# Normalising x on ScalarE instead of VectorE in the attention rounds of an attention and soft-mixture-of-experts kernel

## The reference

```python
def _layernorm(x, axis=-1, eps=1e-05):
    m = jnp.mean(x, axis=axis, keepdims=True)
    v = jnp.var(x, axis=axis, keepdims=True)
    return (x - m) / jnp.sqrt(v + eps)

# attention on the normalised x; each row of the scores is divided by its own length
qkv = einsum('bnm,om->bno', xn, w_qkv)
dots = einsum('bhid,bhjd->bhij', q, k)
attn = dots / max(sqrt(sum(dots * dots, -1)), 1e-12) * norm_g + norm_b
out = einsum('bhij,bhjd->bhid', attn, v) @ w_out.T + b_out
x = x + _layernorm(out)
x = x + _layernorm(soft_moe(_layernorm(x)))
```

## Time and profile before

| what | value |
|---|---|
| runs, us | 905.89, 907.99, 1957.71 |
| median, us | 907.99 |
| span of the profiled execution, us | 906.5 |
| PE busy, share of the span | 95% |
| DVE busy | 69% |
| ACT busy | 55% |
| attention rounds 2 to 6, length of each, us | 20.96 |

### The profile page before, as it was taken

How to read it: one execution, slowest core, us unless ns; L and a number is a source line. 1 busy time by engine, 2 the same in 40 slices (tenths; PEclk the granted TensorE clock), 3 DMA queues, 4 the chain that set the end, 5 groups by cost and what they waited for, 6 DMA issues and landing times.

```text
span 906.5 us, 15936 instructions
## 1 busy us (share of the span) xinstructions
PE 860.1 (95%) x5336; PEld 761.2 (84%) x5336; DVE 629.0 (69%) x1368; ACT 499.3 (55%) x875; POOL 131.4 (14%) x107
## 2 busy tenths in 40 slices
PE   5999999878999999997999999999999999998895
PEld 4888888766888888886899999999999999998895
DVE  4888888668989899998454545453535453479997
ACT  5433333226767667776655555555555554566652
POOL 0011111114322333324000000000000000014422
PEclk9999999969999999999999999999999999999998
DMA  7011120004222222222320202020202020067652
GB/s 245 1 48 47 46 69 23 23 24 162 83 94 105 93 93 93 93 82 82 140 94 1 93 1 94 0 93 0 93 0 93 0 93 1 1 236 275 217 201 93
DMA packets 52231, 75.27 MB, mean 83 GB/s; under 512 B 3040, under 2 KB 33376, under 8 KB 52064
## 3 DMA queue, kind: packets, MB, share of 16 engines
q1 hardware_dynamic: 52192, 74.76, 23.9%
HBM read 49.59 MB, written 25.17 MB: 82 GB/s over the span
## 4 chain that ended last, share of the span: by engine, by line
PE 86%; DVE 9%; ACT 2%; DMA 2%; issue 1%; SPq 0%; DVEq 0%; ACTq 0%
PE bank L847 20%; PE bank L830 19%; PE bank L730 9%; PE bank L755 8%; PE bank L880 7%; DVE comb_r L1636 3%; PE bank L661 3%; PE bank L739 3%; PE bank L613 3%; PE bank L574 2%; PE bank L586 2%; PE bank L645 2%; PE bank L596 2%; PE bank L635 1%; PE bank L625 1%; DMA comb_odd<-combine_scratch 1%
## 5 line engine op out<-in xcount | busy, mean ns | idle before, releaser
L1615 DVE TENSOR_TENSOR act_r<-act,act_r 128x512 fp32r<-128x512 f32 x128 | 88.7, 693 | 188.5 <-ACT act_r L1138 188.5
L847 PEld LDWEIGHTS bank<-w_r,act_r 128*128 128x128 f32 x1536 | 200.8, 191 | 11.8 <-DVE act_r L1615 1.5
L847 PE MATMUL bank<-w_r,act_r 128*128 128x256 f32 x1536 | 204.0, 283 | 1.1 <-DVE act_r L1615 1.1
L830 PE MATMUL bank<-sl_r,w_r 128*128 128x512 f32 x768 | 199.7, 396 | 3.6 <-DVE sl_r L1595 3.6
L1133 ACT ACTIVATE act<-bank,b_sb 128x512 f32<-128x512 f32 x128 | 87.9, 687 | 152.8 <-PE bank L830 152.8
L830 PEld LDWEIGHTS bank<-sl_r,w_r 128*128 128x128 f32 x768 | 137.4, 191 | 26.9 <-issue 4.0
L755 PE MATMUL bank<-disp_r,y_r 128*128 128x512 f32 x384 | 103.6, 406 | 1.0 <-DVE disp_r L1523 0.9
L880 PE MATMUL bank<-eo_r,comb_r 128*128 128x258 f32 x768 | 96.3, 284 | 8.7 <-DVE comb_r L1636 8.7
L880 PEld LDWEIGHTS bank<-eo_r,comb_r 128*128 128x128 f32 x768 | 93.1, 189 | 11.8 <-DVE comb_r L1636 11.4
L730 PE MATMUL bank<-yT_r,snT 128*128 128x512 f32 x384 | 99.0, 393 | 1.2 <-DVE neg_lt L1490 1.2
L730 PEld LDWEIGHTS bank<-yT_r,snT 128*128 128x128 f32 x384 | 71.6, 188 | 16.9 <-issue 1.6
(11 more groups left out here) (143 smaller groups left out, 1184.2 us busy)
## 6 DMA issues: line engine op xcount, KB each, us to landing
stage<-in_w SPq DMA_DIRECT2D x16, 1024.0 KB, 6.7
combine_scratch<-comb SPq DMA_DIRECT2D x64, 256.0 KB, 2.0
stage<-combine_scratch SPq DMA_DIRECT2D x4, 2048.0 KB, 9.0
comb_odd<-combine_scratch SPq DMA_DIRECT2D x4, 2048.0 KB, 9.0
slots_eo<-in_x SPq DMA_DIRECT2D x8, 512.0 KB, 4.2
x_scratch<-stage SPq DMA_DIRECT2D x8, 512.0 KB, 3.0
x<-x_scratch SPq DMA_DIRECT2D x8, 512.0 KB, 3.9
x_d<-x_scratch SPq DMA_DIRECT2D x8, 512.0 KB, 6.8
```

The source lines that it names most:

```text
L830: last = pe.matmul(bank[i % RING][:, :], w1_r[q][:, a, k, j * P:(j + 1) * P], sl_r[f][:, c, k, :], start=(n == 0), stop=(n == len(steps) - 1))
L847: last = pe.matmul(bank[4 + 2 * f + c // 2][:, (c % 2) * D:(c % 2 + 1) * D], act_r[:, i % RING, a, c * S:(c + 1) * S], w2_r[q][:, w, j, :] ...
L1615: v.tensor_tensor(act_r[:, i % RING, 1, :], act[:, i % 2, :], act_r[:, i % RING, 0, :].bitcast(F32), ALU.subtract).then_inc(h_split, 1)
```

## The change

ACT takes over the four instructions that write xn. For that the normalisation is written as `identity(rstd * x + shift)` with `shift = -mean * rstd`; DVE computes `shift` (128x4) right behind the reciprocal. On ACT, `norm_x` stands between the copy of the product of the Gram matrix and the weights (`keep_cw`) and the rounding (`round_xn`). To have `rstd` and `shift` in time, ACT's `root_x` is moved from behind `round_oT` to ahead of it, and DVE's `invert_x_std` (now with the `shift` instruction) from behind `rest_of_oT` to ahead of it.

```diff
+            shift = sb("shift", [P, NT])
+        x_shift = sem("x_shift")
 # ScalarE
+            def norm_x(b, first=False):
+                sc.wait_ge(x_shift, b + 1)
+                if not first:
+                    sc.wait_ge(xnT_in_psum, b * KD)
+                    sc.wait_ge(xn_split, b)
+                alone(sc)
+                for t in range(NT):
+                    last = act_fn(xn[:, t:t + 1, :], x_rows(b, t, 1), ACT.Identity, scale=rstd[:, t:t + 1],
+                                  bias=shift[:, t:t + 1])
+                last.then_inc(xn_ready, 1)
...
+                if following:
+                    root_x(b + 1)
                 if back:
                     round_oT(b - 1, first_back)
                 if first_y:
                     round_yT(0, first=True, at=0)
-                if following:
-                    root_x(b + 1)
                 if front:
                     keep_cw(b, not back)
                 if following:
+                    norm_x(b + 1)
                     round_xn(b + 1)
...
             root_x(0)
+            norm_x(0, first=True)
             round_xn(0, first=True)
 # VectorE
             def invert_x_std(b):
                 dve.wait_ge(x_std, b + 1)
                 v.reciprocal(rstd[:], rstd[:]).then_inc(x_rstd, 1)
-
-            def norm_x(b, first=False):
-
                 dve.wait_ge(x_rstd, b + 1)
-                if not first:
-                    dve.wait_ge(xnT_in_psum, b * KD)
-                    dve.wait_ge(xn_split, b)
-                for t in range(NT):
-                    last = v.tensor_scalar(xn[:, t:t + 1, :], x_rows(b, t, 1), mv[:, t, 0:1], rstd[:, t:t + 1],
-                                           ALU.subtract, ALU.mult)
-                last.then_inc(xn_ready, 1)
+                v.scalar_tensor_tensor(out=shift[:], in0=mv[:, :, 0], scalar=-1.0, in1=rstd[:],
+                                       op0=ALU.mult, op1=ALU.mult).then_inc(x_shift, 1)
...
                 if following:
                     stats_of_x(b + 1)
+                if following:
+                    invert_x_std(b + 1)
                 if back:
                     rest_of_oT(b - 1)
...
-                if following:
-                    invert_x_std(b + 1)
-                    norm_x(b + 1)
                 if end:
                     stats_of_x2(b - 2)
...
             invert_x_std(0)
-            norm_x(0, first=True)
             rest_of_xn(0)
```

## The result

The changed kernel takes 910.74 us (median of 6 runs, 910.2 to 912.6), the kernel before 907.38 (6 runs that include those shown above). The ratio is 1.0040, with a 95% interval of 1.0027 to 1.0053: slower, clear of the noise and far from 2%. Between the two medians lie 3.4 us, but the six runs of before include the disturbed one of 1957.71; without it their median is 906.77, the difference 4.0, and the ratio is taken without it too. Predicted were 911.0 us in a range of 906.5 to 915.0. The profiled execution has a span of 908.5 us, against 906.5.

What follows compares the result with a forecast made beforehand. TensorE, 95% busy and without a gap in round 5, was taken as the bound. The span of 906.5 us plus six stalls of 0.68 (4.1) gave 910.6; with the runs' mean 0.4 above, 911.0, range 906.5 to 915.0.

Steps and rivals of the forecast that it cites:

- The bound and the free DVE time: Whole kernel: TensorE sets the end, so removing four DVE instructions, 1.39 us in round 5, gains 0 us.
- The stall at the projection: Before L661 in rounds 1 to 6: TensorE waits 0.68 us for oT_split, between 0.44 and 0.95.
- three links of the sum: Round 5: shift 0.20 us after the reciprocal starts; 0.17 idle before L1336, both engines arriving together; no catching up.
- The catching up: At L661: TensorE might recover 0.24 us between load and matmul from idle, making the stall 0.44; set aside.
- Six rounds, 4.1 us: Rounds 1 to 6 each lose 0.68 us, 4.1 us together, between 2.6 and 5.7.
- The opening: Batches 0 and 1 before the rounds: 0 us added, at most 0.7.
- The four on ACT: Four 128x256 instructions writing xn on ScalarE: 0.565 us each, 1.96 us together, bounds 1.6 and 2.4.
- The cover behind it: Behind the four on ScalarE: L1280 still ends 0.38 us before TensorE releases keep_heads, so cost 0.
- The price without it: Without the stall, heads come 0.30 us later than before, making a stall of 0.2 per round at L645.
- the rival that rested on it: No stall at the projection, only the heads' 0.2 us in six rounds: 1.2 us, so 908; chance 0.10.
- a rival that came in by half: Hand-over behind the last full round: less half-clock time, 4 to 6 us come back, 905 to 907; chance 0.08.
- The rounds' clock: Short idle times leave TensorE's clock up in the rounds; rival that it falls: 925 or over 930, chance 0.03.

Runs made afterwards that it cites:

- root_only: Kernel before with only root_x moved ahead of round_oT on ScalarE, VectorE's order unchanged; 912.42 us, ratio 1.0045.
- norm_only: Changed kernel with only the move of root_x and invert_x_std undone, the four instructions staying on ScalarE; 907.34 us, ratio 1.0004.
- move_only: Kernel before with only root_x and the reciprocal moved ahead, xn still written by VectorE, no shift; 912.33 us, ratio 1.0050.
- norm_twice: Changed kernel with the four ScalarE instructions issued once more into a tile that nothing reads; 924.99 us, ratio 1.0201.

## Why the prediction was right, point by point

**The bound and the free DVE time: right.** DVE lost four instructions of 1.39 us in each round and nothing became faster. In the experiment with the move undone DVE idles 1.97 us ahead of L1287 and the time is that of before.

**The stall at the projection: right in place; its size, 0.68 us in round 5, is right in part by luck.** The move makes TensorE wait for `oT_split` as predicted, but three links of the sum were mis-sized. The first does not count, since ACT sets the stall; the two others offset each other:

- The shift followed the reciprocal after 0.04 us, not 0.20. (By the prediction's own numbers it would also end at 126.43 and not 126.45.)
- DVE's idle 0.17 ahead of L1336, which I let pass while DVE waited for ACT, stands behind that wait: ACT's first half is done at about 128.40 + 0.69 = 129.09, and DVE starts at 129.35. So ACT's way alone sets the stall, where I had both arrive together; root_only shows it. DVE starts 1.27 us behind its statistics, where I had 126.62 - 125.55 = 1.07: 0.20 too early.
- The catching up that I set aside as seen in no row is there. The first weight load and the first matmul of the projection both start at 130.81, where the load used to come 0.24 ahead. Against the load TensorE is about 0.91 us late (2.73 us behind the statistics, where it was 127.37 - 125.55 = 1.82), and 0.24 of it is recovered.

The later start (0.20) and the recovered 0.24 nearly cancel. With the first alone the sum would have been 0.9 for a round, with the second alone 0.44.

**Six rounds, 4.1 us: 3.9 measured.** The Gram products of batches 1 and 7 are 159.03 - 29.17 = 129.86 us apart; in the kernel before it was 155.05 - 29.07 = 125.98 (the chain of waits). Rounds 3 to 6 lose 0.72 each. Rounds 1 and 2 lose less, 0.4 and 0.6 (21.60 and 21.55 long, before 21.19 and 20.96). I took round 5 for all six. But DVE starts L1343 0.10 and 0.11 us behind ACT's first half in rounds 1 and 2, and 0.26 behind it in rounds 3 to 6; in the kernel before, the idle 0.17 ahead of L1336 is missing in rounds 1 and 2 as well. Why, no run here shows.

**The opening: 0 predicted, at most 0.7.** Batch 1's Gram product starts 0.10 us later than before in the changed kernel (29.17 against 29.07) and 0.35 later in norm_only (29.42).

**The four on ACT: 1.96 predicted, 2.07 measured** (591 ns each, not 565). The prediction's estimate from the Trainium skill's page "ScalarE: Activation LUTs", section "What ACT_TABLE_LOAD costs", was 2.06, and the trace agrees. The rule of the same page of the Trainium skill, section "Rules for kernel authors", that additions and multiplications belong on VectorE, the faster per element, fits the durations (1.39 us there), but a reader who took it for the kernel's time would have been misled here: norm_only has the work on ScalarE at 1.0004.

**The cover behind it: 0.38 predicted, 0.42 measured. The price without it: wrong.** I named 0.2 us per round at L645 when the stall goes away, and gave the rival that rested on it 0.10. norm_only loses nothing. The step that failed is that `qGq` comes later by as much as the heads do. The start of DVE's round stands 3.55 us behind TensorE's head products, and the idle time of 0.53 us ahead of it shrinks to 0.19 to 0.28 when the heads are late.

**The hand-over: a rival that came in by half.** Its half-clock stretch did shorten in the profiled execution. Busy time by stretch, the figure behind POOL's being the granted clock, for the changed kernel:

```profile
184.00:186.00 2.00, 1.32 (x12) 1.13 (x11) 1.90 (x8) 0.30 (x1) 0.00 (x0) 1.00 0.00 0
```

Before, the clock was at 1.2 GHz in the same two microseconds, and by the stretches around it from about 180 to 197 us; here TensorE stays at 2.4 GHz until 188 and is back there at 198.5. Three of its rows:

```profile
183.27 2.05 PE L637 MATMUL bank<-heads,qT 128*128 128x128 f32 x16 [1.90 <-DVE stage L1355]
186.36 1.95 PE L647 MATMUL bank<-head_sel,qGq 128*128 128x8 f32 x16 [1.04 <-DVE qGq L1317]
...
194.58 4.84 PE L663 MATMUL bank<-wout_r,oT_r 128*128 128x256 f32 x24 [1.69 <-DVE oT_r L1343]
```

The kernel before, in the same places, with the same wait of 1.90 us ahead of the first:

```profile
179.34 3.04 PE L635 MATMUL bank<-heads,qT 128*128 128x128 f32 x16 [1.90 <-DVE stage L1348]
182.44 3.58 PE L645 MATMUL bank<-head_sel,qGq 128*128 128x8 f32 x16
```

The changed kernel enters 183.27 - 179.34 = 3.93 us late and is at the logits 199.26 - 197.45 = 1.81 us late. That is why the two profiled spans differ by 2.0 us only. It isn't a merit of the change: the executions of the kernel before differ among themselves by as much. Of its 30 in the experiments, those with a mean granted clock of 0.985 or 0.986 have a median of 908.0 us (11 executions), those with 0.989 one of 906.6 (16; three lie between). The profiled execution of before has 0.985. root_only's has 0.985 too, with the same waits in the hand-over and the same long stretch at 1.2 GHz; move_only's and norm_only's have 0.989 and a stretch of some 10 us, as the changed kernel's. The changed kernel's four executions at 0.989 have 910.4, so like for like the loss is 3.8 us, about what the rounds lose. The groups are small, and before's are not all of one chip. What decides which kind an execution becomes no run here shows.

**The rounds' clock: as predicted.** Idle times of 0.5 us in every round leave it at 1.00 over the rounds (29 to 177 us). What the prediction says of short gaps holds for the rounds only: in the hand-over of the kernel before no idle time of TensorE is longer than 1.90 us, and the clock is at 1.2 GHz for 17 us.

## What to carry to other kernels

Where one engine is busy without a gap, count how early each signal comes that it takes from the others; a move matters only through these covers (0.24 us here), whatever it does to the busy time of an engine that has time to spare. A short instruction that waits for late data must not stand ahead of work that is ready: on an engine that takes its list in order, the root of 0.3 us held up outputs that were there 0.8 us earlier. A sum that comes out right is not yet an account: here two errors of about 0.2 us a round cancelled, and only the rows of the load and of DVE's start show it. And look for the engine's time where it is on the path: 2.7 us of DVE work cost nothing in the wait of round 7 and 3.2 us in the hand-over.

## What the runs showed of the hardware

An idle time that the profile calls issue is not a fixed price. In the rounds read (4 and 5), the first instruction of DVE's next round starts 3.55 or 3.56 us behind the start of TensorE's head products in eight of the nine traces; the idle time ahead of it is 0.52 or 0.53 us where the heads are early and 0.19 to 0.29 where they are late. In norm_twice, where DVE comes later still, it is gone and the round starts 125.88 - 121.53 = 4.35 us behind them. The idle time ahead of L1336 is another kind: where DVE waits for ACT's rounded half, it starts 0.10 to 0.26 us behind the end of that half (rounds 1 and 5 of the changed kernel).

Where TensorE starts the projection from idle, its first weight load and its first matmul start together (130.81 in the changed kernel, 130.90 in root_only); in a round without a gap the load is 0.24 us ahead (127.37 and 127.61 before).

TensorE's clock fell at different places of the hand-over with the same idle times ahead of it. With 0.38 and 1.90 us idle it was at 1.2 GHz from 180 us in the execution of before, less than 1 us into the product behind them, and in the changed kernel's only 5 us into what followed, after a further 1.04 us idle.
